# Twelve decoder sublayers on one core: bf16 constants through TensorE in the waits between stages, and one ScalarE table load moved

## What is computed

```python
x = x + L0_attn(ln(x));   x = x + L0_xattn(ln(x), ctx);  x = x + L0_ffn(ln(x))    # experts, routed by capacity
x = x + L1_attn(ln(x));   x = x + L1_xattn(ln(x), ctx);  x = x + L1_ffn(ln(x))    # two local-attention layers
x = x + L2_attn(ln(x));   x = x + L2_xattn(ln(x), ctx);  x = x + L2_ffn(ln(x))    # experts, top 2
x = x + L3_attn(ln(x));   x = x + L3_xattn(ctx, ln(x));  x = x + L3_ffn(ln(x))    # experts, capacity 1.25
```

## Time and profile before

| | |
|---|---|
| median of 3 runs | 1294.38 us (1293.86 to 1295.42) |
| profiled execution | 1295.03 us |
| its span | 1293.2 us |
| mean granted TensorE clock | 0.933 |
| TensorE matmul busy | 1132.5 us (88%) |
| VectorE busy | 687.4 us (53%) |
| ScalarE busy | 535.4 us (41%) |
| POOL busy | 472.1 us (37%) |

### The profile page before, as it was taken

One profiled execution on the slowest core, in us unless ns is written; L12 is line 12 of the kernel. 1 busy time (PEld: TensorE's weight loads), 2 busy tenths in 40 slices (PEclk: granted clock), 3 DMA queues, 4 the chain that ended last, 5 costly groups with the idle time before them and its releaser, 6 DMA issues. The chain is left out here.

```text
span 1293.2 us, 22659 instructions
## 1 busy us (share of the span) xinstructions
PE 1132.5 (88%) x8669; PEld 789.4 (61%) x8670; DVE 687.4 (53%) x2110; ACT 535.4 (41%) x1374; POOL 472.1 (37%) x547
## 2 busy tenths in 40 slices
PE   5999988999868775898789889989999999978987
PEld 4877766677642243466466646655567775556765
DVE  5555543344359835576467548728833137845413
ACT  5534332466456632345335434314443333443332
POOL 7969630123355522674467450012000003031404
PEclk9999989999895678899999989999989999988989
DMA  5000140522049001000000000001021100010212
GB/s 174 1 5 2 43 169 25 156 66 67 1 155 228 1 2 42 0 2 1 1 1 1 1 9 2 2 1 34 2 73 33 33 32 1 1 37 21 109 39 55
DMA packets 51627, 52.52 MB, mean 41 GB/s; under 512 B 19552, under 2 KB 42336, under 8 KB 50496
## 3 DMA queue, kind: packets, MB, share of 16 engines
q1 hardware_dynamic: 50496, 48.97, 12.1%
q0 software_dynamic: 1024, 2.10, 0.7%
HBM read 43.85 MB, written 7.21 MB: 39 GB/s over the span
## 5 line engine op out<-in xcount | busy, mean ns | idle before, releaser
L471 POOL TENSOR_TENSOR ln_rstd<-ln_ve,ln_half 128x4 f32<-128x4 f32 x28 | 28.5, 1019 | 294.2 <-DVE ln_ve L446 294.0
L659 ACT ACTIVATE scratch<-bank 128x512 f32<-128x512 f32 x96 | 52.3, 595 | 76.7 <-PE bank L555 76.7
L2979 POOL TENSOR_TENSOR scratch<-scratch 128x16 f32<-128x16 f32 x16 | 51.7, 3231 | 50.3 <-DVE scratch L3322 50.3
L614 DVE TENSOR_REDUCE scratch<-bank 128x4 f32<-128x512 f32 x96 | 61.5, 682 | 13.5 <-PE bank L2723 7.7
L1247 ACT ACTIVATE scratch<-bank 128x512 f32<-128x512 f32 x64 | 37.9, 597 | 66.7 <-PE bank L1203 66.7
L2058 POOL TENSOR_TENSOR scratch<-scratch 128x512 f32<-128x512 f32 x32 | 33.2, 1040 | 87.7 <-DVE scratch L2238 87.7
L1213 PEld LDWEIGHTS bank<-weights,scratch 128*128 128x128 f32 x512 | 59.5, 192 | 7.2 <-issue 6.9
L620 DVE TENSOR_TENSOR scratch<-bank,scratch 128x512 f32<-128x512 f32 x96 | 61.3, 680 | 0.0
L1266 DVE SCALAR_TENSOR_TENSOR x_res<-bank,scratch,x_res 128x128 f32<-128x128 f32 x64 | 18.0, 344 | 80.7 <-PE bank L1213 80.7
L1203 PE MATMUL bank<-xnT,weights 128*128 128x512 f32 x128 | 59.5, 608 | 0.7 <-ACT xnT L1236 0.7
L1213 PE MATMUL bank<-weights,scratch 128*128 128x128 f32 x512 | 59.6, 275 | 0.0
(11 more groups left out here) (591 smaller groups left out, 2931.6 us busy)
## 6 DMA issues: line engine op xcount, KB each, us to landing
scratch<-conv_kernels SPq DMA_DIRECT2D x8, 1024.0 KB, 11.0
weights<-e_l_ffn_w SPq DMA_DIRECT2D x20, 256.0 KB, 2.9
scratch<-e_l_ffn_w SPq DMA_DIRECT2D x4, 1024.0 KB, 14.4
values<-scratch SPq DMA_DIRECT2D x8, 512.0 KB, 3.3
scratch<-values SPq DMA_DIRECT2D x8, 512.0 KB, 4.4
weights<-w_l_ffn SPq DMA_DIRECT2D x1, 3698.0 KB, 12.5
scratch<-e_l_ffn_w SPq DMA_DIRECT2D x4, 768.0 KB, 7.0
weights<-w_l_attn SPq DMA_DIRECT2D x1, 2560.5 KB, 8.8
```

What stands on the lines that cost most here:

```text
L614: self.nc.vector.tensor_reduce(self.top[:, n % 4, :], self.by_head(self.core.ps[n % 4][:, :]), AX_X, ALU.max, negate=True).then_inc(self.t ...
L659: self.nc.scalar.activation(self.prob_of(n), self.by_head(self.core.ps[4 + n % 2][:, :]), ACT.Exp, scale=scale) \
L2979: nc.gpsimd.tensor_tensor(rn, ss, power, ALU.pow).then_inc(rooted.sem, rooted.up())
```

## The change

TensorE gets 123 more bf16 matmuls of constants (L134), each group placed in its program ahead of a wait. No other matmul is moved. In `layer_l2_attn` ScalarE copies the first half of `xnT` before it loads the exponential's table, where it loaded the table first. One counter of `layer_l3_ffn` gets a semaphore of its own under another name.

```diff
@@ SmallHeads.pe (steps p of layer_l2_xattn and layer_l3_attn)
             if 0 <= p < self.STEPS:
                 self.pe_turn(pe, p)
+            if p > self.STEPS:
+                self.core.keep_clock_bf(0, 2)
             if p % 2 == 0 and 0 <= (p - 4) // 2 < B:
...
             if p % 2 == 0 and 0 <= (p - 4) // 2 < B:
+                if p > self.STEPS:
+                    self.core.keep_clock_bf(0, 1)
                 self.pe_project(pe, (p - 4) // 2, 7)
+        self.core.keep_clock_bf(0, 2)
@@ layer_l3_ffn
-    load = core.count("rows_loaded")
+    load = core.count("experts_loaded")
@@ layer_l0_ffn
             core.keep_clock(2, 2)
+            core.keep_clock_bf(2, 6)
             pe.wait_ge(chosen.sem, chosen.at(0))
...
             nc.tensor.matmul(ps[3][:, 0:64], tri, flat(mask), start=True, stop=True).then_inc(counted.sem, counted.up())
+            core.keep_clock_bf(4, 4)
             for b in range(B):
@@ layer_l1_attn
             core.keep_clock(O_BANKS[0], 2)
+            core.keep_clock_bf(O_BANKS[0], 4)
             norm.pe(pe, 0, O_BANKS[0])
+            core.keep_clock_bf(O_BANKS[1], 3)
             pe.wait_ge(x_out.sem, x_out.at(0))
@@ layer_l3_xattn
+                if s == -1:
+                    core.keep_clock_bf(0, 11)
                 if 0 <= s + 1 < STEPS:
                     pe.wait_ge(made_normed.sem, made_normed.at(s + 1))
...
+                if s == STEPS:
+                    core.keep_clock_bf(0, 3)
                 if 0 <= s - 1 < STEPS:
                     pe.wait_ge(divided.sem, divided.at(s - 1))
...
+                if s == STEPS - 1:
+                    core.keep_clock_bf(5, 5)
                 if 0 <= s < STEPS:
                     for h in range(H):
                         pe.wait_ge(shifted.sem, shifted.at(2 * s + h))
...
                 if 0 <= s - 1 < STEPS:
+                    if s == STEPS:
+                        core.keep_clock_bf(0, 1)
                     pe.wait_ge(outT.sem, outT.at(s - 1))
...
+            core.keep_clock_bf(0, 3)
@@ layer_l2_attn, TensorE
             norm.pe(pe, 0, 0)
+            core.keep_clock_bf(7, 2)
             pe.wait_ge(*core.w_loaded[tag])
@@ layer_l2_attn, ScalarE
+            act.wait_ge(norm.turned.sem, norm.turned.at(0))
+            nc.scalar.copy(core.xnT[:, half(0)], ps[0][:, :]).then_inc(x_out.sem, x_out.up())
             core.load_table(ACT.Exp)
             act.wait_ge(*core.w_loaded[tag])
-            act.wait_ge(norm.turned.sem, norm.turned.at(0))
-            nc.scalar.copy(core.xnT[:, half(0)], ps[0][:, :]).then_inc(x_out.sem, x_out.up())
@@ layer_l1_ffn
                     turn_qk(g)
+                    if s == 0 and d > 0:
+                        core.keep_clock_bf(O_BANKS[1], 7)
                     if s + 2 < B:
                         project(d, s + 2, 0)
...
                 hand(d, 7, LAST_BANK)
+                core.keep_clock_bf(O_BANKS[0], 6)
                 down(d, 0)
                 hand(d, 8, LAST_BANK)
             for i in range(CHUNKS):
                 up(DEPTH - 1, 1, i)
+            core.keep_clock_bf(0, 5)
             down(DEPTH - 1, 1)
+            core.keep_clock_bf(0, 3)
@@ top_attention
+                    if b >= LAST - 3:
+                        core.keep_clock_bf(7, 4)
                     if b < LAST:
                         pe.wait_ge(kept.sem, kept.at(b))
...
+            core.keep_clock_bf(7, 6)
@@ state_space_out
             for h in range(2):
+                if h == 0:
+                    core.keep_clock_bf(0, 16)
                 mid.pe(pe, h, 6 + h)
+                if h == 0:
+                    core.keep_clock_bf(0, 2)
                 pe.wait_ge(x_out.sem, x_out.at(h))
```

## The result

The changed kernel takes **1275.8 us** (median of 4 runs, 1275.4 to 1276.4), the kernel before on the same chip 1294.9 us (4 runs, 1293.9 to 1298.8). The ratio is 0.985, with a 95% interval from 0.983 to 0.987. The forecast was 1277 us. The time and the sum came out right; of the single terms several did not, as the stages show.

What follows compares the result with a forecast made beforehand. TensorE's clock falling at waits was taken to slow the matmuls behind. Joints' 24.1 us, plus 0.5 for the table, less 0.6 and 1.0 for fillers, gave 23.0, cut to 17.8: 1295.03 to 1277 us, range 1268 to 1289.

Steps and rivals of the forecast that it cites:

- L1203: End of cross layer 2, start of expert layer 2: eight records and transposes at full clock save 2.1 us.
- the end of latent cross attention: L2437 with its followers saves 1.2 us, L1420 and transposes 2.2 us, if the clock stays up.
- Relative attention and the table: `layer_l2_attn`: matmuls at full instead of half clock save 3.1 us; copying xnT before ScalarE's table load saves 0.5 us.
- Gather of `layer_l0_ffn`: Routing of expert layer 0: L1646's 16 records drop from 6.86 to 3.83 us, saving 3.0 us.
- start of `layer_l1_attn`: Attention layer 1: L2083's six records, 4.54 us, take 2.8 us at full clock; 1.5 us counted.
- The eleven: Latent cross attention: matmuls behind eleven fillers speed up, an estimated saving of 1.3 us.
- `top_attention`: Of sixteen fillers before the last four batches' transposes, the last four may push the tail; a loss of 1 us.
- The deductions, one sixth and the halves: Half of L1203's 1.65 and L1420's 1.7 us off, then one sixth for joints that miss: 23.0 to 21.3 to 17.8.
- Second halves that stay low: Rival: clock rises only for the first part of each long low stretch; result near 1287 us; chance 0.22.
- Transposes that do not hold the clock: Rival: mostly-transpose joints (end of cross layer 2, latent cross attention) gain nothing; 1282 us; chance 0.08.
- The slower rival: Constants do not lift the clock and delay `top_attention`'s last four batches; about 1300 us; chance 0.05.
- no change: Rival: waits on VectorE and POOL take up the joints' gains; 1294 us; chance 0.05.

Runs made afterwards that it cites:

- Thin fillers: Changed kernel with its 123 added matmuls each 8 columns wide instead of 512; 1301.3 us, ratio 0.996 to the kernel before.
- table-alone kernel: Kernel before with only ScalarE's first xnT copy moved ahead of the table load, no added matmuls; 1298.9 us, ratio 0.995.
- fillers-only kernel: Changed kernel with the table load back ahead of ScalarE's first copy in relative attention, all 123 fillers kept; 1281.8 us, ratio 0.990.
- local-attention-alone kernel: Kernel before with only the 21 fillers of local attention (`layer_l1_ffn`); 1296.6 us, ratio 0.995.

## Why the prediction was right, and where its steps were not

**The main claim holds.** The clock behind the waits was the quantity to follow, full-sized constants hold it up, and they cost nothing inside idle time. The six joints of the next two paragraphs gave 18.6 us of the 19.6; all other places together gave 1.0 us, as the sum of gains and losses of up to 2 us each. That these nearly cancel, and that the flat deductions come close to what the failed terms missed, is luck. Thin fillers gave nothing, doubled ones cost at least what their ends stick out, and the groups of local attention (5.4 us, tried alone) and of the feed-forward part (3.1 us, removed) acted at their own joints.

**Convolution, its feed-forward part, local attention, L1203, the end of latent cross attention.** Terms 2.4, 2.0, 5.3, 2.1 and 3.4; measured 2.75, 2.2, 4.7, 2.3 and 3.3. The slow group minus the same group at full clock was the right price. (At the convolution 0.8 us came in two traces without any filler there.) The halving for L1203 and L1420, "behind a second short wait of their own", was not needed: few fillers were enough.

**Relative attention and the table.** The sum, 3.6, is right (3.3), the split is wrong. "I take 0.5 us" for the table priced the copy's earlier start on ScalarE alone. The table's move alone brought 3.3 us (2.0 by the other trace of the old order), because the wait on TensorE shrank from 1.44 to 0.77 us and the clock did not fall. The fillers alone bring nearly the same. The step that failed is to price the two as independent.

**Gather of `layer_l0_ffn`, 3.0 us, and start of `layer_l1_attn`, 1.5 us.** These two failed. The gather gave 1.8 us, but gave 1.0 and 1.6 also without fillers, so the 1.8 are not shown to be theirs. The attention's start became 2.0 us slower, since the low level came earlier (L1691, at 218 us, already takes 3.71 us), onto constants that stand ahead of the transposes. "At full clock every one of these fits" was true and not enough: here they ran at the low level, and seven of them stuck out by 1.6 us. I had that price (0.43 us) and used it only as a bound. The seven are not the whole of it either: the table-alone kernel, which has none, lost 2.3 us here. (The row behind the 0.43 us, a pair in 1.06 us, does not give it without an assumption; the changed kernel's six at the low level, 2.77 us, less that pair, do: 0.43 us each.)

**The eleven, 1.3 us.** Nothing came in this measurement. They fill 2.3 us by their price, and the trace shows 2.5 us still idle behind them, at a place where others gained 1.7 us with the same eleven.

**`top_attention`, a loss of 1 us.** Measured 0.6, through the constants that I named. That they also shorten the low stretch was not in the term.

**The deductions, one sixth and the halves, 5.2 us.** They were put in for "joints that miss", and they covered 3.0 - 1.8, 1.5 + 2.0 and 1.3 us, 6 in all. What I did not foresee is that untouched places move as well: the middle of `layer_l1_attn` gained 1.45, the start of `layer_l3_attn` 1.7, two others lost 1.0 and 0.5. Part of this is no effect of the change at all: the 1.45 and the 1.0 appear in the same size in the table-alone kernel, whose program up to there is the old one, and the 1.7 us are missing in the second execution of the changed kernel. "New low stretches where there were none", named as the danger, did appear, as at 218 us, but there also without the change.

**Rivals.** Second halves that stay low: at the joints that were priced it shows in one place, the gather. Transposes that do not hold the clock: groups of transposes behind constants ran fast (L2424 0.66 us, four of L477 0.60 us), and the parts with mostly transposes gave their gain. By the Trainium skill's rule ("TensorE: Matmul & The Clock Gate", Part 4: PE-mode transpose), that transposes do not count as activity like other matmuls, they would not have; the measurement disagrees in its effect, not necessarily in its mechanism, since matmuls lie between. In the 3.4 us that the prediction names, transposes take about 2.7 us, the rest is other matmuls. The slower rival and no change are excluded by the interval.

## What to carry to other kernels

Where a tuned kernel shows matmul groups of one shape with two durations, subtract the fast from the slow one, joint by joint: that is what a few full-width constants ahead of the wait can give, and the number of them is the idle time over 0.21 us, less one or two. Price them at the low level too wherever they stand directly ahead of work that is already released, and do not credit single places from one profile: the low stretches lay elsewhere in stages that nobody touched, and even in two executions of one program. A second trace of the kernel before would have shown that ahead of any change. Look also for what another engine does ahead of the copy that TensorE waits for; taking 0.6 us out of such a wait was worth 2 to 3.3 us.

## What the runs showed of the hardware that I had not expected

**A third level of the clock.** In the fillers-only kernel's profiled execution (1290.2 us, its other three 1279.2 to 1283.9) the granted clock was at 0.95 wherever the other traces have 1.00, over the whole execution; the level of 0.50 occurred beside it as usual. Two windows of it, in which TensorE was busy all the time:

```profile
800.00:850.00 50.00, 50.00 (x580) 33.01 (x580) 26.32 (x50) 15.70 (x29) 0.00 (x0) 0.95 0.01 2
1080.00:1120.00 40.00, 40.00 (x350) 22.11 (x346) 31.29 (x59) 15.48 (x31) 7.65 (x6) 0.95 0.01 1
```

It is no fault of the record: from 944 to 1000 us, nearly all of it TensorE's work, this execution lost 3.0 us on the kernel before, some 5%, and the changed kernel nothing. No other trace shows it, and this kernel's other three runs had mean clocks of 0.949 to 0.953 where this one had 0.912, so it belongs to that run, not to the kernel. Its cause is not known.

**The same gap, two outcomes.** Behind 2.54 us of idle time the same transposes took 1.11 us in one kernel and 0.66 in another, with the same program around them; and behind 1.44 us at the start of relative attention the values (L2670) took 1.90 us in the kernel before and 1.39 in the local-attention-alone kernel. Length of the wait alone does not decide.

**The work, not the instruction.** Sixteen matmuls of 8 columns took 0.55 us and changed nothing; fifteen records of 512 columns took 3.40 us and held the clock.
